# Transpose mode for the matmuls that turn the running maximum back

## The reference

```python
deg     = segment_sum(ones, dst)
agg_sum = segment_sum(x[src], dst)
out1    = batch_norm(x @ W_self1 + (agg_sum / maximum(deg, 1)) @ W_neigh1)
hp      = relu(x @ W_pool + b_pool)
agg_max = segment_max(hp[src], dst)
out2    = batch_norm(x @ W_self2 + agg_max @ W_neigh2)
x       = layernorm(x + leaky_relu(out1 + out2))
```

## Time and profile before

| | us |
|---|---|
| time before, median of 3 runs | 4438.12 (4435.52 to 4441.56) |
| the profiled execution | 4438.06 |
| its span | 4436.3 |
| first pass, first gather to last `ends` (line 1028) | about 8 to 2219 |
| node stage | about 2219 to 2337 |
| second pass and end | about 2337 to 4436 |

### The profile page before, as it was taken

One profiled execution on the slowest core, in us unless ns is written; L12 is line 12 of the kernel. 1 busy time (PEld: TensorE's weight loads), 2 busy tenths in 40 slices (PEclk: granted clock), 3 DMA queues, 4 the chain that ended last, 5 costly groups with the idle time before them and its releaser, 6 DMA issues.

```text
span 4436.3 us, 109751 instructions
## 1 busy us (share of the span) xinstructions
PE 4362.1 (98%) x32762; PEld 3921.0 (88%) x32762; DVE 2229.0 (50%) x5236; ACT 1420.3 (32%) x3823; POOL 3123.4 (70%) x3252
## 2 busy tenths in 40 slices
PE   8999999999999999999989999999999999999996
PEld 7989899999999898989858999999999999999996
DVE  5444444444444444444455555555555555555556
ACT  3333333333333333333243333333333333333333
POOL 7776776777766767667517777777777777777774
PEclk9999999999999999999989999999999999999997
DMA  3111111111111111111124444444444444444442
GB/s 88 38 36 36 36 36 36 36 37 36 37 36 36 37 36 36 36 36 37 27 63 119 116 116 116 116 117 114 117 116 116 116 117 115 116 117 117 116 116 78
DMA packets 209077, 333.35 MB, mean 75 GB/s; under 512 B 73181, under 2 KB 156824, under 8 KB 208952
## 3 DMA queue, kind: packets, MB, share of 16 engines
q0 software_dynamic: 129040, 238.05, 22.6%
q1 hardware_dynamic: 80008, 94.94, 6.9%
HBM read 325.49 MB, written 7.24 MB: 75 GB/s over the span
## 4 chain that ended last, share of the span: by engine, by line
PE 96%; DVE 1%; issue 1%; POOL 1%; ACT 0%; DMA 0%; SPq 0%; POOLq 0%; ACTq 0%; DVEq 0%
PE bank L1019 17%; PE bank L1143 9%; PE bank L1121 9%; PE bank L1129 9%; PE bank L1138 8%; PE bank L988 8%; PE bank L999 8%; PE bank L1160 8%; PE bank L1010 6%; PE bank L1028 6%; PE bank L990 4%; PE bank L1152 1%; POOL kvg L394 1%; PE bank L1069 1%; PE bank L1070 1%
## 5 line engine op out<-in xcount | busy, mean ns | idle before, releaser
L394 POOL DMA_INDIRECT kvg<-in_x_dram,idx x1613 | 1538.0, 954 | 648.4 <-issue 638.7
L394 POOL DMA_INDIRECT kvg<-kv_table,idx x1613 | 1557.6, 966 | 509.0 <-issue 459.9
L1019 PE MATMUL bank<-ident,scan 96*128 96x96 f32 x3232 | 832.0, 400 | 0.0
L667 DVE TENSOR_TENSOR acc<-acc,bank 97x64 f32 (+1 forms) x808 | 177.5, 220 | 1244.7 <-PE bank L1010 949.9
L1019 PEld LDWEIGHTS bank<-ident,scan 96*128 96x128 f32 x3232 | 787.3, 328 | 0.0
L551 ACT COPY eaC<-bank 96x512 f32<-96x512 f32 x404 | 234.7, 581 | 1119.2 <-PE bank L1121 1108.7
L473 ACT COPY scanE<-bank 128x384 f32<-128x384 f32 x404 | 193.1, 478 | 1225.5 <-PE bank L1019 1225.5
L1028 PEld LDWEIGHTS bank<-S,scanE 128*96 128x96 f32 x3232 | 339.6, 165 | 216.0 <-issue 214.0
L657 DVE TENSOR_TENSOR_SCAN scan<-keepC,scan,bank 96x512 f32<-96x512 bf16 x404 | 513.1, 1270 | 0.0
L642 DVE TENSOR_TENSOR S<-iotaW,rel 128x512 f32<-128x512 f32 (+1 forms) x808 | 445.8, 552 | 25.5 <-issue 25.5
L1143 PE MATMUL bank<-qwin,scan 64*128 64x96 f32 x3232 | 456.0, 281 | 0.0
(11 more groups left out here) (125 smaller groups left out, 5038.4 us busy)
## 6 DMA issues: line engine op xcount, KB each, us to landing
ea<-in_edge_attr_dram SPq DMA_DIRECT2D x402, 192.0 KB, 2.5
kvg<-in_x_dram,idx POOLq DMA_INDIRECT x1613, 2.5
kvg<-kv_table,idx POOLq DMA_INDIRECT x1613
kv_table<-stage SPq DMA_DIRECT2D x6, 672.0 KB, 3.3
stage<-counts_row SPq DMA_DIRECT2D x1, 2352.0 KB, 12.9
xN<-in_x_dram SPq DMA_DIRECT2D x6, 336.0 KB, 3.3
out_dram<-xN SPq DMA_DIRECT2D x6, 336.0 KB
src_all<-in_src_groups_dram SPq DMA_DIRECT2D x1, 804.0 KB
```

What stands on the lines that cost most here:

```text
L394: pool.indirect_dma_start(out=to[:, r, j, :], out_offset=None, in_=table, in_offset=bass.IndirectOffsetOnAxis(ap=idx[:, r, j:j + 1], axis= ...
L1019: last = pe.matmul(bank[4 + b][:, j * D:(j + 1) * D], scan[:, b, j:GE:J], ident[0:D, 0:D], start=True, stop=True)
```

## The change

The four plain matmuls against the identity in `back` become four transposes with the same operands: the same stationary operand, the same identity, the same output. Nothing else changes; the other identity matmuls of both passes (lines 988, 990, 1121, 1129) stay plain. On every engine the instructions stand in the same order as before. Code behind line 1019 moves up by one line, so line 1028 is line 1027 in the changed kernel.

```diff
@@ -1016,8 +1016,7 @@
                     pe.wait_ge(s_scan, ready(i, r))
                     pe.wait_ge(s_bcp, freed(i, r, 2))
                     for j in range(J):
-                        last = pe.matmul(bank[4 + b][:, j * D:(j + 1) * D], scan[:, b, j:GE:J], ident[0:D, 0:D],
-                                         start=True, stop=True)
+                        last = pe.transpose(bank[4 + b][:, j * D:(j + 1) * D], scan[:, b, j:GE:J], ident[0:D, 0:D])
                     last.then_inc(s_back, 1)
```

## The result

The changed kernel takes **4337.53 us** (median of 4 runs, 4333.28 to 4342.89) against 4439.34 us for the kernel before (4 runs, 4435.52 to 4441.56): a ratio of 0.977, 95% interval 0.9755 to 0.9789. The forecast was 4269 us with a range of 4252 to 4315, so the time lies outside it: faster, as forecast, but by 102 us and not by 169. The profiled execution took 4333.28 us, its span is 4331.6.

A forecast was written before the change was run, and what follows sets the result against it. The prediction took PE to bound the first pass at 5.41 us a group, with POOL next at 4.99. Its terms, -155.2 and -13.8 us, sum to -169.0 us from 4438.06: 4269 us, range 4252 to 4315.

The forecast's parts named there:

- The bound moves from PE to POOL: First pass: PE's group falls from 5.41 to 4.46 us, so POOL's 4.99 us of gathers sets the pace; 81%.
- PE stays the bound: Rival: PE still bounds the first pass and the whole 384 us come, 4054 us; 3%.
- Price of a tile: One transpose in `back` costs 0.2375 us instead of 0.475, between 0.11 and 0.475 us.
- Term 1: First pass, POOL's 1,595 gather steps after the 18th gather: 1.251 us each, 1995.3 us instead of 2150.5, -155.2 us.
- if a gather's step changes once PE no longer paces it: One of the signs named in advance that would show the forecast wrong; no size or chance given.
- clock, mild: Rival: PE's clock low for 25 to 35% of the pass, or a PE-DVE-ACT wait, 4312 to 4430 us; 8%.
- Term 2: End of the first pass, last gather's start to the last `ends`: 17.3 us instead of 31.1, -13.8 us.
- Node stage and second pass at 0: Both keep their instructions and only start earlier: 0 us.
- The clock: First pass: PE's granted clock may fall as PE idles 0.5 of 5 us, but the ring of four covers it.
- The range: Whole kernel: 4252 to 4315 us, leaving out the 19% of the rivals.

The follow-up runs named there:

- experiment 4: Changed kernel plus three plain matmuls per first-pass group at the end of PE's step, ahead of the running maximum's transposes: 4326.3 us, repeated 4332.4 us.
- experiment 6: Changed kernel with DVE's line 642 put ahead of the second window sum in its step, nothing left out: 4264.7 us.
- experiment 8: Changed kernel with the second pass's identity matmuls of edge features and S as transposes: 5362.8 us; edge features alone 4338.1, S alone 4350.1 us.
- experiment 2: Changed kernel with DVE's scan (line 657) cut to the first 128 of 512 columns from turn 7 on: 4327.6 us.

## Why the prediction was right and wrong

- **The bound moves from PE to POOL: right.** POOL has no idle over 0.3 us, PE waits 300.0 us for gathers, and 0.66 us more PE work in a group costs nothing (experiment 4). The rival "PE stays the bound", 4054 us, is out.
- **Price of a tile: wrong size, no effect.** I took 0.2375 us, it is 0.12 us, near the lower bound: not only is there one load for a tile and not two, it is also shorter than each of the two was (218 ns against 328). As the text said, between 0.11 and 0.37 us it makes no difference; it only let PE idle more than the 0.5 us a group that I wrote (1,798 - 1,497.46 us for some 347 groups is 0.87 us).
- **Term 1, 1,595 steps of POOL: the step that failed.** It took a gather's 0.947 us from a stretch in which PE set the pace of both POOL and DVE. In that state gathers and line 642 stand at fixed places against each other, and few starts fall into line 642 (24 of 1,578 gathers over 1.0 us from 60 to 2190 us, by the timeline). Once POOL sets the pace and DVE's step follows the landing of the gathers, they meet: 220 of 1,576. The gather that I had at 0.947 us took 0.990, the idle between two stayed at 0.30. The term came out at -83.7 us instead of -155.2. The second pass's mean, 0.966 us, which I used only as the upper end, was already a sign of the same thing: there, too, a gather that starts 0.1 us after line 642 takes 1.14 us on the mean, against 0.95 for one that starts at the same time or before. I named "where more of DVE's work lies beside the gathers" and did not ask which of its instructions and at what distance. My last sentence named the sign, "if a gather's step changes once PE no longer paces it", and that is what came; but none of the rivals was made of it and it had no chance of its own. The measured time lies in the range of the rival "clock, mild" (4312 to 4430 us) by its number alone: that rival's causes were the clock, which was 0.98, or a wait between PE, DVE and ACT, and the hold is one between DVE and POOL.
- **Term 2, the end of the pass: right in its size**, -14.1 against -13.8 us, with some luck. The last `front` follows the last gather after 5.4 us (forecast 5.7), and from there it is the 11.6 us that I wrote. But a `back` saves 4 x (0.475 - 0.12) = 1.42 us and not 0.95, so three of them should have taken 4.3 us off today's 14.4; only 2.8 went, for PE comes to wait there (0.24 us for the scan at 2112.46).
- **Node stage and second pass at 0: right within 6 us**, the node stage took 5.3 us less, with a granted clock of 0.90 on its mean against 0.82.
- **The clock: right.** Falls come (0.98 on the mean) and are covered; experiment 4 shows that they are free.
- **The range: wrong.** Its upper end came from the second pass's step of 1.271 us or from the clock; the hold makes the step 1.296 us, 2% more than 1.271. With what I had, the bound should have been worked out from the worst phase: were one gather of each group held by 0.47 us, the longest mean of the table, it would be 404 x 0.47 = 190 us (an estimate), more than the whole gain of 169 us that I forecast. This number could be read from the trace of before: its 24 gathers over 1.0 us are 1.09 to 1.46 us long.

## What to carry to other kernels

When a change moves the bound from one engine to another, the new bound's instruction lengths have to be taken from a stretch in which it already sets the pace, and the worst of its lengths, not the mean, prices the risk: two engines that kept a fixed distance while a third set the pace need not keep it afterwards. An instruction on an engine that is off the path can hold another engine's instruction, and whether it does depends on its start time; moving it by 0.9 us (experiment 6) was worth some 70 us and cost nothing. And a transpose-mode matmul is cheap for PE but is not a free substitute: look at the granted clock of the stretch before and after (1.00 and 0.50 in experiment 8).

## What the runs showed of the hardware

- **A DVE tensor_tensor with two operands in SBUF holds a gather that POOL starts meanwhile.** 0.94 us become 1.41 on the mean where it starts 0.1 us behind line 642; the gather ends 0.82 us after line 642 does. The scan, which reads one operand from SBUF and one from PSUM, does not hold it, nor does line 877, a tensor_tensor with one operand in PSUM; line 901, as long and with both in SBUF, does (experiment 2). The Trainium skill, page "SBUF — State Buffer", section "Who interferes with whom", says that a DVE instruction with two SBUF inputs contends with a GpSimd instruction that reads SBUF, and in its section "Summary: rules for kernel authors" that the second one to issue blocks in full until the first finishes. The table above agrees: a gather that starts first is not touched, one that starts second waits for the end. The first of these sections also tells of a probe in which a tensor_tensor did not stall a DMA; here tensor_tensors do hold POOL's part of one, by 0.47 us in the table's longest row, and the measurement decides. That the ports are the cause is the page's account; no run here moved an operand of line 642 out of SBUF.
- **Transposes of fp32 data have one record where a matmul has two**, and a tile whose stationary operand has a step of four elements costs 0.12 us against 0.475 us.
- **Transposes can keep the clock down**: 0.50 in a pass in which PE was busy without a gap (experiment 8). The Trainium skill, page "TensorE: Matmul & The Clock Gate", section "Part 4: PE-mode transpose", says that a transpose does not count as PE-busy in the same way and that the full clock does not engage for it. Experiment 8 with both kinds transposed agrees in direction (0.50 with PE busy without a gap); with one kind, and in the first pass of the changed kernel, four transposes in each group leave the clock at 0.98. The page "Perfetto Trace Analysis", section "Transposes", advises to write every logical transpose as a transpose; experiment 8 speaks against that as a rule: it is 1,025 us slower than the changed kernel.
